# Wide attention on Trainium2: one pair of PSUM banks for the scores and two pairs for the turned scores

## What is computed

```python
# layer 1, feed-forward: 8 heads, the values chosen among 8 experts by the gate
gm = jax.nn.one_hot(argmax(gates), EXPERTS) * gates
values = jnp.einsum('bhne,ehdk,bnd->bhnk', gm, value_experts, x)
attn = softmax(where(causal_mask, finfo.min, einsum('bhid,bhjd->bhij', q * SCALE, k)))
out = jnp.einsum('bhij,bhjk->bhik', attn, values)
out = jnp.einsum('bhne,ehkd,bhnk->bhnd', gm, output_experts, out).sum(axis=1)
# layer 2, attention: 16 heads, keys and values from one projection
q = (x @ w_q) / sqrt(d);  kv = x @ w_kv;  k = kv * (1.0 + k_weights)
a = softmax(where(tril, einsum('bhik,bhjk->bhij', q, k), -1e6))
y = einsum('bhij,bhjv->bhiv', a, kv) @ w_o
```

## Time and profile before

| | |
|---|---|
| time, median of 3 runs | 3728.91 us (3724.46 to 3735.41) |
| the profiled execution's own time | 3724.0 us |
| its span, first to last instruction | 3722.1 us |
| mean granted TensorE clock | 0.887 |
| PE busy | 2911.5 us (78%) |
| DVE busy | 2148.3 us (58%) |
| ACT busy | 1263.5 us (34%) |
| POOL busy | 794.8 us (21%) |
| reduces of `skv_negmax` (L1822), 128 | 104.1 us, VectorE idle before them 135.4 us |
| exponentials into `skv_probs` (L1863), 128 | 90.0 us, ScalarE idle before them 220.7 us |

### The profile page before, as it was taken

The page is one execution under the profiler, slowest core; times in us unless marked ns, Lnnn a source line. Parts: engine busy times, 40 slices in busy tenths (PEclk is TensorE's granted clock), DMA queues, the critical chain, the costliest instruction groups (busy, mean ns, idle before and its releaser), DMA issues. The chain is left out here.

```text
span 3722.1 us, 42867 instructions
## 1 busy us (share of the span) xinstructions
PE 2911.5 (78%) x15553; PEld 1420.5 (38%) x15600; DVE 2148.3 (58%) x4210; ACT 1263.5 (34%) x2179; POOL 794.8 (21%) x950
## 2 busy tenths in 40 slices
PE   4996879555667987878778876878696499799998
PEld 1332334111213544454535443434343223244555
DVE  5884821777885554555454445454656688554444
ACT  2664622333333521202110212212263166445222
POOL 1201100544661002111020413224203310010000
PEclk9997989777888988989898989989797599899999
DMA  5212100100003100000000000000210122130000
GB/s 130 40 27 68 34 17 1 45 0 0 1 0 65 32 1 1 1 1 1 1 1 16 1 1 1 1 1 1 41 29 0 18 47 40 54 61 12 1 1 12
DMA packets 39985, 74.76 MB, mean 20 GB/s; under 512 B 13048, under 2 KB 31916, under 8 KB 35936
## 3 DMA queue, kind: packets, MB, share of 16 engines
q1 hardware_dynamic: 39776, 72.03, 8.9%
HBM read 26.34 MB, written 1.05 MB: 7 GB/s over the span
## 5 line engine op out<-in xcount | busy, mean ns | idle before, releaser
L1619 POOL TENSOR_TENSOR mamba_dbu<-mamba_du,mamba_b 128x512 f32<-128x512 f32 x128 | 255.9, 2031 | 132.5 <-ACT mamba_b L1602 132.5
L1586 PE MATMUL ps<-mamba_hc,weights 128*128 128x512 f32 x256 | 165.4, 738 | 98.5 <-DVE mamba_hc L1644 98.1
L1633 DVE TENSOR_TENSOR_SCAN mamba_h<-mamba_da,mamba_dbu 128x512 f32<-128x512 f32 x128 | 211.0, 1651 | 18.3 <-ACT mamba_da L1607 18.3
L534 DVE TENSOR_REDUCE L3a_negmax<-ps 128x1 f32<-128x512 f32 x256 | 162.3, 683 | 52.0 <-PE ps L294 33.7
L534 DVE TENSOR_REDUCE L0a_negmax<-ps 128x1 f32<-128x512 f32 x256 | 162.4, 683 | 50.2 <-PE ps L294 45.7
L164 POOL TENSOR_SCALAR vareps<-mv 128x4 f32<-128x4 f32 x24 | 6.0, 252 | 863.8 <-DVE mv L1260 452.3
L1822 DVE TENSOR_REDUCE skv_negmax<-ps 128x2 f32<-128x256 f32 (+3 forms) x128 | 104.1, 823 | 135.4 <-PE ps L1686 133.4
L397 ACT ACTIVATE L0a_probs<-ps 128x512 f32<-128x512 f32 x256 | 143.6, 599 | 76.2 <-PE ps L313 65.1
L397 ACT ACTIVATE L3a_probs<-ps 128x512 f32<-128x512 f32 x256 | 143.7, 600 | 73.5 <-PE ps L313 62.5
L1863 ACT ACTIVATE skv_probs<-ps 128x1024 f32<-128x1024 f32 (+3 forms) x128 | 90.0, 703 | 220.7 <-PE ps L1686 209.4
L2029 PE MATMUL ps<-stream,moa_xm 128*128 128x128 f32 x1024 | 161.8, 306 | 1.4 <-DVE moa_xm L2051 1.4
(11 more groups left out here) (618 smaller groups left out, 6832.0 us busy)
## 6 DMA issues: line engine op xcount, KB each, us to landing
stream<-stream SPq DMA_DIRECT2D x32, 192.0 KB
stream<-gate_up_down_in SPq DMA_DIRECT2D x1, 4352.0 KB, 12.9
stream<-value_output_in SPq DMA_DIRECT2D x1, 4096.0 KB, 12.3
stream<-ffn_in SPq DMA_DIRECT2D x1, 2888.0 KB, 10.0
L0a_qs<-L0a_qs SPq DMA_DIRECT2D x16, 128.0 KB
L0x_qs<-L0x_qs SPq DMA_DIRECT2D x16, 128.0 KB
L1x_qs<-L1x_qs SPq DMA_DIRECT2D x16, 128.0 KB
L2x_qs<-L2x_qs SPq DMA_DIRECT2D x16, 128.0 KB
```

Source lines behind the costliest of these rows:

```text
L534: dve.tensor_reduce(negmax[:, hh // G % 4, a, hh % G:hh % G + 1], ps[:, i % S_RING, :], AX.X, ALU.max, negate=True).then_inc(s["maxed"], 1)
L1586: pe.matmul(ps[:, 4 + j, :], k.ident, hc[:, (J * n + j) % RING, :], start=n == 0, stop=n == N - 1).then_inc(s["summed"], 1)
L1619: pool.tensor_tensor(dbu[:, i % RING, :], du[:, j, :], bsb[:, n % AHEAD, :], ALU.mult).then_inc(s["dbu_ready"], 1)
L1633: dve.tensor_tensor_scan(out=hs[:, i % RING, :], data0=da[:, i % RING, :], data1=dbu[:, i % RING, :], initial=0.0, op0=ALU.mult, op1=ALU.a ...
```

## The change

The scores get one pair of banks, 0 and 1, for all blocks. The turned scores get two pairs, (2, 3) for even blocks and (4, 5) for odd ones. So `scores` waits for the reduce of the block just before it, from the second block on, and `scores_turned` waits for the exponential of two blocks before, from the third on. The reduce and the exponential read the banks accordingly. The order of the work on every engine, the number of instructions and their shapes stay.

```diff
--- before.py
+++ after.py
@@ -1674,7 +1674,7 @@
     inv = sb("inv", [P, SEQ], F32)
     halves, tri, triT, sel = (wb(k, n).rearrange("p (c n) -> p c n", c=2) for n in ("halves", "tri", "triT", "sel"))
     ones = w(k, "const", "one")
-    S_BANK, T_BANK, Z_BANK, M_BANK = (0, 2), 4, 6, 7
+    S_BANK, T_BANK, Z_BANK, M_BANK = 0, (2, 4), 6, 7
     mt_ps = ps[:, M_BANK, :].bitcast(BF16)
 
     with phase(k, "chain", "cleared", "scores", "maxed", "split", "mt_ready", "mt_sb", "scoresT", "exped", "weighed",
@@ -1688,15 +1688,15 @@
 
             def scores(r, qt):
                 i = r * NT + qt
-                if i >= 2:
-
-                    pe.wait_ge(s["maxed"], i - 1)
+                if i >= 1:
+
+                    pe.wait_ge(s["maxed"], i)
                 n = (qt + 1) * P
                 for a in range(2):
-                    at, bank = slice(WD * a, WD * a + WD), S_BANK[i % 2] + a
+                    at, bank = slice(WD * a, WD * a + WD), S_BANK + a
                     pe.matmul(ps[:, bank, 0:n], qT[at, r, qt * P:n], kT[at, r, 0:n], start=True, stop=True)
                 for a in range(2):
-                    at, bank = slice(WD * a, WD * a + WD), S_BANK[i % 2] + a
+                    at, bank = slice(WD * a, WD * a + WD), S_BANK + a
                     last = masked(ps[:, bank, qt * P:n], at, tri)
                 last.then_inc(s["scores"], 1)
 
@@ -1718,18 +1718,19 @@
                 if r % G == 0 and t == 0:
                     pe.wait_ge(s["mt_sb"], g + 1)
                 i = r * NT + t
-                if i >= 1:
-
-                    pe.wait_ge(s["exped"], i)
+                if i >= 2:
+
+                    pe.wait_ge(s["exped"], i - 1)
                 q0 = t * P
+                bank = T_BANK[i % 2]
                 for a in range(2):
                     at = slice(WD * a, WD * a + WD)
-                    pe.matmul(ps[:, T_BANK + a, q0:], kT[at, r, q0:q0 + P], qT[at, r, q0:], start=True, stop=False)
+                    pe.matmul(ps[:, bank + a, q0:], kT[at, r, q0:q0 + P], qT[at, r, q0:], start=True, stop=False)
                 for a in range(2):
                     at = slice(WD * a, WD * a + WD)
-                    pe.matmul(ps[:, T_BANK + a, q0:], sel[at, r % G, :], mt[at, g % 2, q0:], start=False, stop=True)
+                    pe.matmul(ps[:, bank + a, q0:], sel[at, r % G, :], mt[at, g % 2, q0:], start=False, stop=True)
                 for a in range(2):
-                    last = masked(ps[:, T_BANK + a, q0:q0 + P], slice(WD * a, WD * a + WD), triT)
+                    last = masked(ps[:, bank + a, q0:q0 + P], slice(WD * a, WD * a + WD), triT)
                 last.then_inc(s["scoresT"], 1)
 
             def weigh(r):
@@ -1818,8 +1819,7 @@
             def maxima(r, qt):
                 i = r * NT + qt
                 dve.wait_ge(s["scores"], i + 1)
-                b = S_BANK[i % 2]
-                dve.tensor_reduce(negmax[:, qt, 2 * r:2 * r + 2], ps[:, b:b + 2, 0:(qt + 1) * P], AX.X,
+                dve.tensor_reduce(negmax[:, qt, 2 * r:2 * r + 2], ps[:, S_BANK:S_BANK + 2, 0:(qt + 1) * P], AX.X,
                                   ALU.max, negate=True).then_inc(s["maxed"], 1)
 
             def invert(r, t):
@@ -1860,7 +1860,7 @@
                             act.wait_ge(s["weighed"], step - 1)
                             act.wait_ge(s["added"], 2 * (step - 1))
                         act.wait_ge(s["scoresT"], i + 1)
-                        act.activation(probs[:, step % 2, :, t, t * P:], ps[:, T_BANK:T_BANK + 2, t * P:], ACT.Exp,
+                        act.activation(probs[:, step % 2, :, t, t * P:], ps[:, T_BANK[i % 2]:T_BANK[i % 2] + 2, t * P:], ACT.Exp,
                                        scale=scale).then_inc(s["exped"], 1)
                     if t == 2 and step >= 1:
 
```

## The result

The changed kernel takes 3811.9 us in the median of four runs, against 3726.9 us for the kernel before on the same chip: 1.0224 times as long, with an interval of 1.0205 to 1.0242. The loss is 85 us; the forecast was 67 and the range reached to 3830.

What follows compares the result with a forecast made beforehand. No engine fills the calls; waits at the seams bound them, on reduces in the fill and exponentials in the tail. Terms 82 + 4 - 47 + 28 = +67 us gave 3792 us, range 3750 to 3830.

Steps and rivals of the forecast that it cites:

- -43, +82 and +28: Eight-call sums: +4 in the middle with -47 in the tail, +82 for fill turn-taking, +28 for slower TensorE.
- The clock: TensorE's granted clock falls in part of the fills: +28 us in all, bounds 0 to +60.
- Taking turns, 7.36 us a fill step: Fill: TensorE and VectorE alternate, 3.68 + 3.28 + 0.40 us a step; +10.3 us a call, +82 in eight.
- A step at the lower clock, 10.4 us: Fill step at 1.2 GHz: score blocks take 6.7 us in place of 3.68, so a step takes 10.4.
- The middle: Steps with score and turned blocks: turned blocks cover most reduces; +4 us in eight calls, bounds 0 and +8.
- the walk: Block-by-block estimate of the first middle step in a shared-key call: 8.05 us against 7.6 shown.
- The holds of 0.5 and 1.1 us at the late reduces: Middle: third reduce delays the last score block by 0.5 us, fourth delays the next step's first by 1.1.
- The +0.45 a call: Net cost of the first middle step, 8.05 us against 7.6, charged to every call.
- The tail: Steps with turned blocks only: plain step falls from 9.30 to 7.07 us; -47 in eight calls, bounds -60 and -33.
- the rival of the slow clock: Clock stays down through every fill and into the first middle step: about +108 us, 3832; chance 0.14.
- the stretch with 4.36 us busy of 8 at 1.00: Profile row cited for the fill: TensorE busy 4.36 of 8 us was still granted clock 1.00.
- the row of 3.21 at 0.50: Profile row cited for the fill: TensorE busy 3.21 of 8 us at clock 0.50 stayed there.

Runs made afterwards that it cites:

- work in the gaps: Changed kernel plus 1, 2, 3 and 4 matmuls into an idle bank behind the four score blocks of each fill step: 3737.8 us, ratio 1.0028.
- the hybrid: Against the kernel before: scores alternate between two bank pairs in the fill only, then use one; turned scores have two: 3661.8 us, ratio 0.9823.
- half the added work: Changed kernel plus 0, 1, 1 and 2 matmuls behind the four score blocks of a fill step, four in place of ten: 3780.8 us, ratio 1.0146.

## Why the prediction was right, and where its sizes were off

The sign, the places and the mechanism hold: twelve blocks a call pay for the lost pair, the tail gains from the new one, and the fill is the larger. The runs divide the result into three parts, each between two neighbours: 3661.8 - 3727.9 = -66 us for the second turned pair, net of the scores' single pair in the middle; 3737.8 - 3661.8 = +76 for taking turns in the fill at the higher clock; 3811.9 - 3737.8 = +74 for the clock. The forecast had -43, +82 and +28. The kernel of 3737.8 us has added work in the gaps, so this division holds only as far as that work costs nothing, which the steps of 7.39 us bear out.

That the total came out 20 us from the forecast owes something to luck. The clock was put 46 us too low and the gain outside the fills 23 too low, and the two errors work against each other. With 74 for the clock and all else as forecast the sum is 3724 + 82 + 4 - 47 + 74 = 3837, outside the range.

- **Taking turns, 7.36 us a fill step.** 7.38 to 7.40 measured, at 1.00. The handovers were about 0.05 us, as taken. Between the fills of the hybrid and those with work in the gaps lie the 82 us of the forecast.
- **A step at the lower clock, 10.4 us.** 10.31 measured.
- **The middle.** For the first step of a shared-key call the walk gave 8.05 us; it is 8.05 in the run with work in the gaps and 8.25 in the hybrid. The holds of 0.5 and 1.1 us at the late reduces are 0.35 and 0.55 to 0.88. The +0.45 a call was wrong for the expert calls: I charged them the late reduce beside T(3), but they have no score block in the next step that could wait for it, and a wait of 0.48 us of T(0) for an exponential, at 1397.51 in the trace of before, went as well. From T(0) to T(0) the step fell from 7.56 to 6.46.
- **The tail.** 7.07 us forecast, 6.97 measured, from 9.30. The tail step with `turn_maxima` was put at a gain of 1.37 and gave 1.81 to 1.84 (9.29 to 7.48, 10.47 to 8.63). With the middle that makes -61 us in the calls where I had -43; two of the four shared-key calls of the kernel before also lost a stretch at the lower clock in their last middle step and the tail step behind it (13.6 and 11.7 us in place of 12.2 and 10.5), which the hybrid does not show in three of its four calls. That part of the -61 is not the tail's own.
- **The clock: the term that failed.** "I take 28" stood between 0 and 60. It is 74: 52 in the fills, within the bound, and the rest outside them, where the sum had nothing and the rival of the slow clock had 1 to 2 us a call. Two things were missed. I let the clock fall in part of the fills, going by the stretch with 4.36 us busy of 8 at 1.00; it is down in all of them, from about the start of the second step in three shared-key calls and from inside the first in the fourth, and stayed down to the end of the fill. And I let the slow stretch end with the fill: it ran on into the first step of the middle, some 16 us in eight calls. The row with 4.36 us was the wrong neighbour; the row of 3.21 at 0.50 was the right one, and those rows did not say which. Of the rivals, the slow clock (3832) was 20 us too high and the forecast 20 too low; the truth was the slow clock's fill with a larger gain outside it.

The Trainium skill, TensorE: Matmul & The Clock Gate, section "A second HAM failure mode: psum-queue depth-cycling", names short rests between matmul groups as enough to throttle the clock. The trace agrees that they suffice, with rests of 0.5 to 1.3 us in each block; it does not show a swing within a fill of the changed kernel but one fall and a long stay. What the Trainium skill reports on the same page, section "HAM oscillation — how this bites in real kernels", that PSUM double-buffering gained next to nothing, does not hold for the fill here: it is worth 150 us between the changed kernel and the hybrid.

What stays open is why the clock rises again in one fill and not in another with the same instructions (25.4 and 30.9 us with half the added work). The runs show that it happens and what it costs, not what decides.

## What to carry to other kernels

When buffers move from one pair of stages to another, ask at each stretch of the pipeline which of the two stages is alone there: a producer with one buffer and nothing else to do takes turns with its reader, and the price is the sum of both, not the longer. A buffer need not belong to one stage; a ring over all blocks in program order gives the fill, the middle and the tail what each can use, and was worth 158 us against the change. Where a change makes TensorE rest in short pieces, price the work at both clock levels and let the lower one run on past the stretch itself.

## What was not expected of the hardware

Matmuls added in the fills made the kernel faster by 74 us, and those added at the calls' ends by some 11, since the matmuls that count then ran at 2.4 GHz for more of the time. The fall came early: the first fill step of a shared-key call is at 1.00 with 3.66 us busy of 7.30, and the next is at 0.50. At 0.50 the profile showed TensorE busy for 13.73 us of 20.60, and in one fill with half the added work for 26.29 of 30.90, and the clock stayed down all the same.
